# A gated-attention and mixture-of-experts block on one core: first expert tiles taken from two groups' rows, and the late expert weights loaded in 18 pieces

## What is computed

```python
x = x + tanh(g_xattn[0]) * xattn(ctx, ctx, layernorm(x), ssm_kernel, D, 8)
xf = layernorm(x)                                      # (2048, 256)
scores = sigmoid(xf @ w_router); sfc = scores + corr_bias
...                                                    # 4 best of 8 groups, then the 6 best experts
combine = zeros((T, 32)).at[rows, topk_idx].add(topk_w)
g = einsum('th,ehm->etm', xf, gate_w); u = einsum('th,ehm->etm', xf, up_w)    # M = 176
eo = einsum('etm,emh->eth', silu(g) * u, down_w)
routed = einsum('te,eth->th', combine, eo)
shared = silu(xf @ sh_gate_w) * (xf @ sh_up_w) @ sh_down_w
x = x + tanh(g_ffn[0]) * (routed + shared)
```

## Time and profile before

| | |
|---|---|
| Median of 3 runs | 551.79 us (551.52 to 555.46) |
| The profiled execution | 550.17 us, its span 548.3 us |
| PE busy | 439.9 us, 80% of the span |
| POOL / DVE / ACT busy | 288.8 / 313.1 / 204.1 us |
| Moved by DMA | 85.38 MB, mean 156 GB/s |

### The profile page before, as it was taken

The page is one execution under the profiler, slowest core; times in us unless marked ns, Lnnn a source line. Parts: engine busy times, 40 slices in busy tenths (PEclk is TensorE's granted clock), DMA queues, the critical chain, the costliest instruction groups (busy, mean ns, idle before and its releaser), DMA issues.

```text
span 548.3 us, 8656 instructions
## 1 busy us (share of the span) xinstructions
PE 439.9 (80%) x2114; PEld 330.0 (60%) x2114; DVE 313.1 (57%) x1163; ACT 204.1 (37%) x522; POOL 288.8 (53%) x224
## 2 busy tenths in 40 slices
PE   0733879788889669465999999999999999999900
PEld 0633757666766547323777777777777777777600
DVE  2999999969968756312444444444444444444307
ACT  3531734443552321001444444444444444444400
POOL 2000018867884751772655566666656566656620
PEclk9985999999969959965999999999999999999965
DMA  7999302222221499984666666666666666666559
GB/s 262 366 307 405 140 18 99 93 91 89 92 104 58 138 259 326 361 288 135 111 105 119 110 114 112 116 112 114 112 115 111 115 113 115 110 119 110 70 141 353
DMA packets 56053, 85.38 MB, mean 156 GB/s; under 512 B 6492, under 2 KB 47676, under 8 KB 55740
## 3 DMA queue, kind: packets, MB, share of 16 engines
q1 hardware_dynamic: 33566, 47.20, 28.8%
q0 software_dynamic: 20160, 28.37, 27.7%
q10 hardware_dynamic: 2270, 9.15, 4.5%
HBM read 44.91 MB, written 39.80 MB: 154 GB/s over the span
## 4 chain that ended last, share of the span: by engine, by line
PE 60%; DVE 20%; another core or an unknown queue 6%; DMA 6%; issue 4%; ACT 2%; POOL 1%; SPq 1%; POOLq 0%; DVEq 0%; ACTq 0%
PE bank L1207 23%; PE bank L1226 16%; DVE arena L658 5%; PE bank L1196 4%; PE bank L1217 4%; PE bank L1069 4%; PE bank L1090 3%; DVE arena L666 2%; PE bank L1040 2%; DVE arena L636 2%; DMA arena<-token_sums 2%; DMA token_sums<-shgu_sb,dest 2%; DMA rows<-x 1%; DVE arena L735 1%
## 5 line engine op out<-in xcount | busy, mean ns | idle before, releaser
L395 POOL DMA_INDIRECT expert_lists<-payload,slots x96 | 116.9, 1217 | 127.3 <-DVE slots L765 84.7
L1207 PE MATMUL bank<-wgu,work 128*128 x432 | 149.8, 470 | 1.6 <-issue 1.6
L1226 PE MATMUL bank<-wd,work 88*128 x432 | 112.1, 382 | 2.6 <-ACT work L561 2.6
L991 DVE TENSOR_TENSOR work<-work,bank 128x176 f32<-128x176 f32 x108 | 36.5, 338 | 129.9 <-ACT work L554 113.6
L1207 PEld LDWEIGHTS bank<-wgu,work 128*128 128x128 f32 x432 | 75.5, 195 | 25.8 <-issue 3.8
L554 ACT ACTIVATE work<-bank 128x176 f32<-128x176 f32 x108 | 34.3, 318 | 122.3 <-PE bank L1207 100.0
L1226 PEld LDWEIGHTS bank<-wd,work 88*128 88x128 f32 x432 | 73.8, 191 | 9.2 <-issue 3.3
L973 DVE COPY work<-bank 128x256 f32<-128x256 f32 x108 | 45.9, 425 | 35.4 <-PE bank L1196 18.8
L410 POOL DMA_INDIRECT token_sums<-q_sb,dest x28 | 43.7, 1559 | 27.1 <-DVE work L985 7.7
L410 POOL DMA_INDIRECT token_sums<-shgu_sb,dest x28 | 43.6, 1559 | 25.6 <-DMA token_sums<-shgu_sb,dest 7.8
L1217 PEld LDWEIGHTS bank<-ident,work 128*88 128x88 f32 x216 | 26.5, 123 | 37.6 <-issue 18.8
(11 more groups left out here) (170 smaller groups left out, 559.3 us busy)
## 6 DMA issues: line engine op xcount, KB each, us to landing
payload<-expert_lists SPq DMA_DIRECT2D x108, 144.5 KB
wgu<-w_gu SPq DMA_DIRECT2D x1, 4928.0 KB, 20.1
wgu<-w_gu ACTq DMA_DIRECT2D x1, 4928.0 KB
expert_lists<-blank SPq DMA_DIRECT2D x1, 4768.5 KB, 25.9
arena<-token_sums SPq DMA_DIRECT2D x8, 512.0 KB, 7.2
wd<-w_down SPq DMA_DIRECT2D x1, 3168.0 KB
token_sums<-blank SPq DMA_DIRECT2D x1, 2304.0 KB, 29.1
out<-arena SPq DMA_DIRECT2D x4, 512.0 KB, 4.9
```

Of the source, the lines that this page charges most:

```text
L395: nc.gpsimd.indirect_dma_start(lists, bass.IndirectOffsetOnAxis(ap=slots[:, g % 2, b, k:k + 1], axis=0), pay[g % 2][:, b, :], None).then_i ...
L1207: last = nc.tensor.matmul(bank[2 + t % 2][:, 0:2 * M], xT_half(t, k), wgu[:, bass.ds(e * WGU_E + k * 2 * M, 2 * M)], start=(k == 0), stop= ...
L1226: last = nc.tensor.matmul(bank[6 + t % 2][:, 0:L], hT_half(t, c), wd[:, bass.ds(e * WD_E + c * L, L)], start=(c == 0), stop=(c == 1))
```

## The change

Four things are changed together.

1. The early tiles are described from two groups instead of three (KNOWN 12 becomes 8, the counts are taken in pass NG - 3), and from 14 experts instead of 18 (EA is EARLY).
2. The first IN_ARENA = 8 of them get a ring of four places of their own in a free end of `arena` (TILES_AT). SP loads them after `tables_a_ready` and `payload_free` of NG - 1, not NG. From tile 8 on, the ring is `payload` again, and the loads wait for `payload_free` of NG as before.
3. SP loads only `wd` of experts 0 to 13 (one transfer). `late_in` is that one alone.
4. `wgu` and `wd` of experts 14 to 31 are loaded by ACT, two experts at a time, in 18 transfers: six of `wgu` in the last pass, one of `wgu` and one of `wd` in each of the ACT steps of tiles 0 to 2, and one of `wd` in each step of tiles 3 to 8. The last two of `wd` lie over the new ring and wait until its eight tiles are through.

```diff
+TILES_AT = ROUTER_AT + KC * E
+assert TILES_AT + 4 * ROW <= ARENA
+WD_TILES = (ROUTER_AT - WD_AT) // WD_E // 2 * 2
+LATE = [n for n in range(EARLY, E, 2)]
+IN_ARENA = 2 * NX
-KNOWN = (NG - 1) * GB
-EA = WD_MID
+KNOWN = (NG - 2) * GB
+EA = EARLY
...
+        tile_rows = lambda t, at, n: (win(arena, TILES_AT + t % NX * ROW + at, [[1, n]]) if t < IN_ARENA
+                                      else payload[:, t % NX, at:at + n])
...
             sp.wait_ge(pairs_summed, 2 * NG)
-            load_down(sp, 0, WD_MID, late_in)
-            load_up(sp, EARLY, WD_MID, late_in)
+            load_down(sp, 0, EARLY, late_in)
+            sp.wait_ge(payload_free, NG - 1)
             sp.wait_ge(tables_a_ready, 1)
+            for t in range(IN_ARENA):
+                load_tile(t)
             sp.wait_ge(payload_free, NG)
-            for t in range(NX):
-                load_tile(t)
-            for t in range(NX, NA):
+            for t in range(IN_ARENA, NA):
                 load_tile(t)
...
+                    if not attend:
+                        act.wait_ge(pairs_summed, 2 * NG)
+                        load_up(act, EARLY, EARLY + 2, last_in)
...
                     if not attend:
-                        load_up(act, WD_MID, E, last_in)
+                        load_up(act, EARLY + 2, EARLY + 4, last_in)
...
+                        if not attend:
+                            load_up(act, EARLY + 4 + 2 * b, EARLY + 6 + 2 * b, last_in)
...
+            def late_weights(t):
+                if t < 3:
+                    n = EARLY + 12 + 2 * t
+                    load_up(act, n, n + 2, last_in)
+                if t < len(LATE):
+                    n = LATE[t]
+                    if n == WD_LAST:
+                        act.wait_ge(sh_stored, 16 * (B - GB))
+                        act.wait_ge(sh_added, GB)
+                    if n == WD_TILES:
+                        act.wait_ge(t_xT, IN_ARENA)
+                        act.wait_ge(t_picked, IN_ARENA)
+                    load_down(act, n, n + 2, last_in)
...
-            load_down(act, WD_MID, WD_LAST, last_in)
-            act.wait_ge(sh_stored, 16 * (B - GB))
-            act.wait_ge(sh_added, GB)
-            load_down(act, WD_LAST, E, last_in)
...
                 if t >= 2:
                     copy_y(t - 2)
+                if t < NA:
+                    late_weights(t)
...
-                    if g == NG - 2:
+                    if g == NG - 3:
                         nc.vector.tensor_copy(count_a[:, :], bank[4][:, 2 * GB * E:(2 * GB + 1) * E])
...
                 if t == NA:
-                    pe.wait_ge(last_in, 48)
+                    pe.wait_ge(last_in, 2 * len(LATE) * 16)
...
-            pe.wait_ge(late_in, 32)
+            pe.wait_ge(late_in, 16)
```

More of the change, by code:

```diff
@@ L59 @@
 ROUTER_AT = SHOUT_AT + 2 * L
-assert ROUTER_AT + KC * E <= ARENA
+TILES_AT = ROUTER_AT + KC * E
+assert TILES_AT + 4 * ROW <= ARENA
 STATS_AT, MOMENTS_AT, NEWTON_AT = TMP_AT, TMP_AT + 6 * B, TMP_AT + 8 * B
@@ L312, in load_tile @@
                 first = table_value(sp, tile_row, t, E * LIST)
-                sp.dma_start(payload[:, t % NX, :], lists[bass.ds(first, P), :]).then_inc(t_loaded[t % NX], 16)
+                sp.dma_start(tile_rows(t, 0, ROW), lists[bass.ds(first, P), :]).then_inc(t_loaded[t % NX], 16)
             def load_block(n):
@@ L977, in pick @@
                 mask = win(work, MASK_AT + t % 2 * E, [[1, E]])
-                nc.vector.scalar_tensor_tensor(mask, iota_e[:, :], tile_e[:, t:t + 1], payload[:, t % NX, SCORE_AT:ROW],
+                nc.vector.scalar_tensor_tensor(mask, iota_e[:, :], tile_e[:, t:t + 1], tile_rows(t, SCORE_AT, E),
                                                ALU.is_equal, ALU.mult).then_inc(t_masked, 1)
@@ L981, in pick @@
                     dve.wait_ge(t_added[t % NX], nth(t - NPICK))
-                nc.vector.tensor_scalar(dest[:, t % NPICK:t % NPICK + 1], payload[:, t % NX, TOK_AT:TOK_AT + 1],
+                nc.vector.tensor_scalar(dest[:, t % NPICK:t % NPICK + 1], tile_rows(t, TOK_AT, 1),
                                         tile_dump[:, t:t + 1], float(t % S * SUM_ROWS), ALU.max, ALU.add)
@@ L1196, in xT @@
                     last = nc.tensor.transpose(bank[t % 2][:, k * P:(k + 1) * P],
-                                               payload[:, t % NX, k * P:(k + 1) * P], ident[:, :])
+                                               tile_rows(t, k * P, P), ident[:, :])
                 last.then_inc(t_xT, 1)
```

## The result

The changed kernel takes 571.52 us (median of 4 runs, 566.71 to 575.97) against 553.28 us (4 runs of the kernel before, 551.52 to 555.46): ratio 1.0288, 95% interval 1.0232 to 1.0345. The prediction was 537 us, faster. Its profiled execution took 568.13 us, with a span of 566.1 us where the kernel before has 548.3. Some profiled executions further down (those of f1, f3, g3 and h4) ran 0.6 to 1.6% longer than their kernel's median, so places and waits are read from them, and no times.

What follows compares the result with a forecast made beforehand. The prediction took PE's own work, 2.49 us a tile, to bound the kernel from 260 us on, after a start 16.9 us too long. Its terms, -3.0 - 1.0 - 16.9 + 6 = -14.9 us, gave 537 us, range 528 to 548.

Steps and rivals of the forecast that it cites:

- What bounds the kernel: From 260 us on only PE's work counts, 2.49 us a tile; the tile stage's start costs 16.9 us more than its tiles.
- Its adds, busy for 1.6 of 2.49 us, catch up: End of the kernel: POOL's adds, not before about 243, make up their delay, so the end is unchanged; nothing.
- The earlier loads: Tiles 0 to 3 load at about 206 instead of 218.85, gaining only what tile 0 waited: 1.0 us, between 0 and 1.94.
- The refill: New ring, tiles 4 to 7: places refilled 10 us ahead of use, at most 1.2 us short once, so nothing.
- Less traffic in the last pass: Fewer weights queued remove the 3.03 us step at 205.73; bounds 0 and 5.4; slots at 206.7, POOL starts at 211.
- The loss: First tiles: late signals while scatters run beside them take back 6 us of the 16.9 gained, between 0 and 12.7.
- Its cause: Stall at the first tiles: signals arrive late while both weights and scatters flow; 16.1 us lost in 19 us of overlap.
- The rule against the row: DMA never contends with a compute engine, so the 13 us stall may have another cause, which the change may remove whole.
- ACT's issues: Last pass and first tile steps: ACT's new issues, 0.57 us or less each, are covered by idle time; cost nothing.
- Late weights hold tile 16: Slower rival: PE waits before tile 16 for the 18 pieces; landing at 300 would give about 563 us; chance 0.04.
- The first rival: No late signals at all at the first tiles: gain 20.9 or 23.3 us, 531 down to 528.5 us; chance 0.22.
- The second rival: The stall only moves with the sooner tiles, 16.1 us lost as before: 4.8 us gained, 547 us; chance 0.13.

Runs made afterwards that it cites:

- f1: The changed kernel, but in the last group POOL waits after every sixth scatter until all have landed; 562.21 us.
- f3: The changed kernel with gate and up weights of experts 16 to 31 in one transfer after the last pass's first silu; 566.43 us.
- g3: The kernel before with one buffer clearing after each last-group scatter, and those scatters started once their slots are known; 537.97 us.
- h4: The changed kernel with one buffer clearing after each last-group scatter, and those scatters started once their slots are known; 556.56 us.
- f4: The changed kernel, but POOL clears a small spare buffer four times after each scatter of the last group; 565.41 us.
- g1: The changed kernel with one clearing of a small spare buffer after each scatter of the last group; 541.78 us.
- e1: The changed kernel without the last group's 24 scatters, its rows left out of the counts, still 108 tiles; 548.56 us.
- e2: The changed kernel with all 18 weight pieces issued in ACT's steps of tiles 4 to 12, none in the last pass; 587.46 us.
- e4: The kernel before with the 18 weight pieces and 14 early experts, the old ring, and tables from three groups; 570.27 us.
- h1: The kernel before, unchanged, run again beside h4; 552.09 us.
- e3: The kernel before with the new ring and the tables from two groups and 14 experts, weights in the old transfers; 555.6 us.
- group g: g1, g3 and two more kernels with the one clearing per last-group scatter, side by side on one chip; the kernel before took 539.5 us there.

## Why the prediction was wrong

The sum had -3.0, -1.0, -16.9 and +6. Its steps, in its own order:

- **What bounds the kernel: incomplete.** "There only PE's own work counts" is true of PE's rate, not of the end. POOL's adds need 2.48 us each, as f4 and g1 show, against PE's 2.49. The end is at least the first add + 107 x 2.48 + 23.2. For the kernel before that gives 256.74 + 265.4 + 23.2 = 545.3 of its 548.3 us: had PE lost nothing in the dip and the first add stayed, 3 us were to be had, not 16.9. It does not say what the change would have gained: with no signal late the first add would have moved too.
- **"Its adds, busy for 1.6 of 2.49 us, catch up": the step that failed in kind.** 1.6 us is how long POOL is busy, not how often it may issue. The trace of the kernel before had it: between 310 and 520 us, 33 of POOL's waits, 34.0 us of idle time, are ended by the landing of an earlier add. I took the idle 0.9 us before each add for slack.
- **The number of tiles: right**, 108.
- **The earlier loads: right in direction**, 210.35 instead of 218.85 (I said 206). **The refill: wrong.** I put it at nothing; in the changed kernel a load into the ring takes 8.71 us in the chain of waits, from 263.00, beside the pieces, and PE waits 2.5 us for it.
- **Less traffic in the last pass: wrong.** The step at 205.73 went, but those ahead of it grew: 1.55 and 2.41 us at 195 and 197, and ACT stood 7.16 us for its scores at 203.30, 4.8 before. The slots came at 212.15 instead of 209.70 (I said 206.7), and POOL began at 217.45 instead of 218.96 (I said 211): group 2's last scatter still landed at 216.4. Taking 3.0 us off had no ground in a row; the zero bound was the better value, and it too was short by 2.5.
- **The loss, put at 6 between 0 and 12.7: the step that failed in place.** I asked how much of the tile stage lies beside scatters, and took the end of pass 3 as safe, for in the kernel before nothing was late there. But there the cast, at 222.44, fell 3.5 us behind the first scatter, and the pass's last signal from PE to DVE, at 227.66, 8.7 us behind; in the changed kernel PE's tables are ready at 227.6, 10 us behind, with two more such steps to come. The delay then hit two signals for which all of the tile stage waits, by 12.7 and 6.2 us. Inside the tile stage, 2.1 us were lost, as the best case had it.
- **Its cause: wrong.** Not "while both flow": e1 (pieces, no scatters) has none of it, e2 (scatters, no pieces) has the longest wait, 21.42 us. The share of 16.1 us lost in 19 us of overlap, from which the bound of 12.7 came, was no property of the traffic.
- **The rule against the row**: the rule that transfers don't hold an engine up agrees with f4, where the same bytes flowed beside working engines. It did not follow that the stall would go, since by f1 and f4 what holds the signals is how POOL issues, and the change left that alone.
- **ACT's issues: right**, no wait is put down to them. **Late weights hold tile 16: right**, they don't; but they have a price that I did not list: 8.8 us on POOL's first 20 adds.
- **The first rival**, no late signals at all, comes nearest in f4, and that took 565.41 us, not 531: its scatters ended so late that the first add came at 271.72. The second rival had the stall move and last as long; what moved was 18.9 us onto pass 3, not 16.1 onto the tiles.

In the kernel before the last scatter (248.14) and the last of the weights in ACT's queue end together with the delay (249.3), so its trace could not tell the two from their sum. The prediction should have had scatters alone as a rival with a chance of its own; by it, a change that only thins out the weights gains nothing.

**What stays open.** How an unbroken run of scatters holds back signals isn't in any trace, only that PE's signals to DVE and ACT come late in it, and that breaks let them through. What of a break does it isn't known either: in h4 the gap between scatters grew only from 0.30 to 0.40 us, but POOL ran another instruction in it and waited for its own semaphore, as in f4. In f1 waits of 3 to 8 us for landings did it without another instruction; a short delay with nothing else in it wasn't run. Nor is settled why the delay begins 8 to 11 us after the first scatter in the changed kernel, e2, e4 and f3, and 13 to 19 us after it in the kernel before, h1 and e3 (counted to the first signal over 2 us late); the pieces' kernels have less traffic then, but f3, made to test that, moved it by no more than a microsecond or two. And in group g the kernel before was 12 to 15 us faster than elsewhere, and in g3, the same kernel with both edits, the slots came at 197 instead of 210. The edits touch nothing before those slots, so on that chip the first three groups' scatters cost nothing of the kind; what was different there isn't known.

## What to carry to other kernels

Before costing a stall at the head of a pipeline, find for each engine how often it may issue in the steady stage, not how long it is busy: two engines here had the same period of 2.5 us, and a gain on PE alone was worth 3 us at most. Where a signal comes late, ask which engine's run begins and ends with the delay, and break that run before moving transfers about. And when a load is moved, look at what it will then flow beside: here the pieces met their own deadline and still made the first adds slower.

## What the hardware showed that was not expected

- POOL's scatters, one every 1.27 us without a break, held back other engines' signals in every group but g: by 12.7 and 6.2 us in the changed kernel, and DVE stood 21.4 us before one cast in e2. With 1.3 us between them instead of 0.3 (f4) the same cast waited 1.56 us. With the 24 issued in sixes, or with two in flight (where it lies beside group 2's scatters), it was 1.32 and 1.56. In h4 a gap of 0.40 us with one clearing in it was enough for the cast (1.86 us), though not for every signal.
- The same issue order in group g cost nothing in passes 1 to 3: slots at 195.5 us in g1, 212.2 in the changed kernel.
- Full queues didn't do it: PE was busy for 9.47 of 10 us at 360 GB/s.
- Indirect adds to DRAM with two in flight run at 2.48 us each (f4, g1), and at 3.00 to 3.26 for the first 20 where the weights' pieces are under way beside them (214 GB/s in h4, 249 in the changed kernel).
